# A DLRM tower with all pair products: 256 of the 780 pairs laid out with samples on partitions, and the batch in five blocks

## What is computed

```
e = stack of tbl_f[ids[:, f]] for the 40 fields          # (2048, 40, 64), f32
vi, vj = e[:, i_idx, :], e[:, j_idx, :]                   # 780 pairs i < j
z = einsum('bpe,bpe->bp', einsum('bpd,pde->bpe', vi, W), vj)
h = concatenate([z, dense_ctx], axis=1)                   # 796 columns
h = maximum(h @ W_top1 + b_top1, 0)                       # 796 -> 512
h = maximum(h @ W_top2 + b_top2, 0)                       # 512 -> 256
y = h @ W_top3                                            # 256 -> 1
```

## Time and profile before

| | before |
|---|---|
| median of 3 runs | 1374.25 us (1374.18 to 1374.57) |
| the profiled execution, its time | 1374.48 us |
| its span, from first to last instruction | 1372.7 us |
| PE busy | 1307.9 us (95%) |
| DVE busy | 928.9 us (68%) |
| POOL busy | 604.8 us (44%) |
| ACT busy | 83.4 us (6%) |
| mean granted TensorE clock | 0.994 of 2.4 GHz |

### The profile page before, as it was taken

The page is one execution under the profiler, slowest core; times in us unless marked ns, Lnnn a source line. Parts: engine busy times, 40 slices in busy tenths (PEclk is TensorE's granted clock), DMA queues, the critical chain, the costliest instruction groups (busy, mean ns, idle before and its releaser), DMA issues.

```text
span 1372.7 us, 17118 instructions
## 1 busy us (share of the span) xinstructions
PE 1307.9 (95%) x7024; PEld 463.4 (34%) x7024; DVE 928.9 (68%) x804; ACT 83.4 (6%) x137; POOL 604.8 (44%) x646
## 2 busy tenths in 40 slices
PE   0699999998999999999999999999999999999998
PEld 0233333332333333333333333333333333333333
DVE  0378877776634788788854588878873478888860
ACT  0000000000000000000000100000000000000001
POOL 6777777777777777754543444451000000000000
PEclk9899999999999999999999999999999999999999
DMA  4233332222222233322211222222110011111100
GB/s 163 42 73 73 70 69 73 73 66 65 65 42 58 66 74 72 74 66 63 65 45 37 47 66 62 62 64 53 47 40 23 23 48 51 50 47 47 32 1 0
DMA packets 49782, 77.38 MB, mean 56 GB/s; under 512 B 13540, under 2 KB 13540, under 8 KB 49576
## 3 DMA queue, kind: packets, MB, share of 16 engines
q1 hardware_dynamic: 29216, 55.26, 13.6%
q0 software_dynamic: 20480, 21.01, 8.4%
q10 hardware_dynamic: 8, 0.01, 0.0%
HBM read 76.22 MB, written 0.01 MB: 56 GB/s over the span
## 4 chain that ended last, share of the span: by engine, by line
PE 86%; POOL 9%; issue 3%; DMA 1%; ACT 1%; POOLq 0%
PE u_ps L311 48%; PE z_ps L328 25%; POOL rows L268 9%; PE turn_ps L342 6%; PE turn_ps L294 3%; PE turn_ps L347 2%; PE u_ps L342 1%; PE u_ps L313 1%; PE u_ps L347 1%; PE turn_ps L351 0%; DMA rows<-in_tbl,ids_all 0%; ACT h_sb L418 0%; DMA ids_all<-in_ids 0%; PE u_ps L351 0%; ACT y_row L424 0%
## 5 line engine op out<-in xcount | busy, mean ns | idle before, releaser
L388 DVE TENSOR_TENSOR prod<-u_ps,x 128x1024 f32<-128x1024 f32 x800 | 928.2, 1218 | 401.8 <-PE u_ps L313 398.4
L313 PE MATMUL u_ps<-x,w_ring 64*128 64x512 f32 x1600 | 759.9, 610 | 0.0
L311 PE MATMUL u_ps<-x,w_ring 64*128 64x512 f32 x1600 | 759.9, 610 | 0.0
L268 POOL DMA_INDIRECT rows<-in_tbl,ids_all x640 | 604.1, 944 | 326.9 <-issue 196.1
L311 PEld LDWEIGHTS u_ps<-x,w_ring 64*128 64x128 f32 x1600 | 279.9, 187 | 420.4 <-issue 324.9
L328 PE MATMUL z_ps<-prod,ones 128*32 128x512 f32 x3200 | 393.4, 601 | 0.0
L313 PEld LDWEIGHTS u_ps<-x,w_ring 64*128 64x128 f32 x1600 | 279.8, 187 | 0.0
L328 PEld LDWEIGHTS z_ps<-prod,ones 128*32 128x32 f32 x3200 | 85.6, 109 | 279.7 <-issue 152.4
L294 PE MATMUL turn_ps<-ident,rows 128*128 128x128 f32 x320 | 53.9, 293 | 60.3 <-DMA rows<-in_tbl,ids_all 54.3
L407 ACT COPY x<-turn_ps 128x512 f32<-128x512 f32 x80 | 46.9, 586 | 635.8 <-PE turn_ps L294 635.8
L342 PE MATMUL turn_ps<-z_sb,mlp_sb 128*128 128x512 f32 x182 | 81.5, 599 | 0.8 <-ACT z_sb L412 0.8
(11 more groups left out here) (19 smaller groups left out, 14.7 us busy)
## 6 DMA issues: line engine op xcount, KB each, us to landing
w_ring<-in_w_pair SPq DMA_DIRECT2D x200, 256.0 KB, 2.7
rows<-in_tbl,ids_all POOLq DMA_INDIRECT x640, 2.5
mlp_sb<-in_mlp SPq DMA_DIRECT2D x1, 2308.0 KB, 11.5
ids_all<-in_ids SPq DMA_DIRECT2D x1, 320.0 KB, 3.3
z_sb<-in_dense_t SPq DMA_DIRECT2D x4, 32.0 KB
out_y<-y_row ACTq DMA_DIRECT2D x4, 2.0 KB
```

The source lines that it names most:

```text
L268: nc.gpsimd.indirect_dma_start(rows[:, slot, s, par * DIM:(par + 1) * DIM], None, tables[f], bass.IndirectOffsetOnAxis(ap=ids_all[:, SUB * ...
L311: pe.matmul(u_ps[:, bank, :], w_ring[0:DIM, c % W_SLOTS, cols], x[0:DIM, b % 2, n_even, :], start=True, stop=True)
L313: pe.matmul(u_ps[:, bank + 1, :], w_ring[DIM:P, c % W_SLOTS, cols], x[DIM:P, b % 2, n, :], start=True, stop=True).then_inc(mains_done, 1)
L388: nc.vector.tensor_tensor(prod[:, full % PROD_SLOTS], u_ps[:, bank:bank + 2, :], other, ALU.mult).then_inc(prods_done, 1)
```

## The change

The batch goes through in five blocks, of 256, 512, 512, 512 and 256 samples. Each block has 136 units as before, called standing (F, and D for the pairs inside duos). The other pairs, those between each of the 16 duos 4 to 19 and the 8 fields of duos 0 to 3, 256 in all, are done in moving units (R). There the operands change places: 128 samples of `x` stand in the array, and the eight matrices of a field, 512 columns, move through. A moving unit does 128 samples and 16 pairs. A block of 512 has 64 of them (four times 16), one of 256 has 32. Its products (L555) are made with the gathered rows themselves, which stay in `kept`, and lie in `rprod` with samples on partitions, so that the sum over the 64 numbers of a field runs along the columns. That sum is one instruction of VectorE (L578), or sixteen of ScalarE with 64 columns each (L614). VectorE takes the first 24 moving units and then every fourth, 82 in all, and ScalarE 174. The 256 sums of a sample are turned around by TensorE in two pieces a block (`zr`, L484), and ScalarE copies them to `z_sb` (L624). TensorE's sums (L473) are left for the standing units, 34 groups a block, and come at least three units after their group. `z_sb` keeps seven chunks (five and two).

`prod` becomes `fprod` (8 slots) and `rprod` (4 slots), `rows` has 6 slots, the weights come through 4 slots for standing and 3 for moving units. `x` is a ring of 28 duos, and 12 duos of the next block are turned within a block. Pieces of the layers lie six units apart.

```diff
-BLOCK = 512
+SIZES = [256, 512, 512, 512, 256]
+KEEP = 4
+X_SLOTS = 28
+WF_SLOTS, WR_SLOTS = 4, 3
+ROW_SLOTS = 6
+FPROD_SLOTS, RPROD_SLOTS = 2 * GROUP, 4
+SUM_LAG = 3
+def block_units(b):
+    moving = [("R", n, s) for n in range(KEEP, DUOS) for s in range(SUBS[b])]
+    ...
+def on_vector(u):
+    r = R_AT[u]
+    return r < 24 or r % 4 == 3
+MLP_AT = {3: ("zr", 0), 5: ("zr", 1), 16: ("l1", 0), 22: ("l1", 1), 28: ("l1", 2), 34: ("l1", 3),
+          40: ("l2", 0), 46: ("l2", 1), 52: ("l3", 0)}
+    free = 116 if b == 0 else 70          # duos_before_unit: the next block's 12 duos
+    for n in range(EARLY_DUOS):
+        at.setdefault(free + (len(UNITS[b]) - 4 - free) * n // EARLY_DUOS, []).append((b + 1, n))
 # TensorE, a unit
+    if kind == "R":
+        op = pe.matmul(u_ps[:, bank + half, :], x[on, x_slot(b, n), k * P:(k + 1) * P],
+                       wr_ring[on, c % WR_SLOTS, :], start=True, stop=True)
 # VectorE, a unit
+    if kind == "R":
+        nc.vector.tensor_tensor(rprod[:, r % RPROD_SLOTS], u_ps[:, bank:bank + 2, :],
+                                kept[:, b % 2, k:k + 1, :].to_broadcast([P, 2, KEPT * DIM]), ALU.mult)
 # VectorE's sum, one product later
+        nc.vector.tensor_reduce(zb[:, s, at:at + 2 * KEPT],
+                                rprod[:, r % RPROD_SLOTS].rearrange("p h (j d) -> p (h j) d", d=DIM),
+                                AX.X, ALU.add).then_inc(vsums_done, 1)
 # ScalarE's sum
+        for j in range(2 * KEPT):
+            one = rprod[:, slot, j // KEPT, j % KEPT * DIM:(j % KEPT + 1) * DIM]
+            op = nc.scalar.activation(one, one, ACT.Copy, accum_out=zb[:, s, at + j:at + j + 1])
+            op.then_inc(asums_done, 1)
```

More of the change, by code:

```diff
@@ L23, with standing_units @@
 BLOCK = 512
-SUB = BLOCK // P
 H1, H2 = 512, 256
 M1, M2 = H1 // P, H2 // P
+SIZES = [256, 512, 512, 512, 256]
+NB = len(SIZES)
+STARTS = [sum(SIZES[:b]) for b in range(NB)]
+SUBS = [n // P for n in SIZES]
+KEEP = 4
+KEPT = 2 * KEEP
 GROUP = 4
-W_SLOTS = 8
-ROW_SLOTS = 10
+X_SLOTS = 28
+WF_SLOTS, WR_SLOTS = 4, 3
+ROW_SLOTS = 6
 U_SLOTS = 3
-PROD_SLOTS = 2 * GROUP
-def unit_list():
-    units = []
+FPROD_SLOTS, RPROD_SLOTS = 2 * GROUP, 4
+SUM_LAG = 3
+def standing_units():
+    out = []
     for n in range(DUOS):
@@ L38, in unit_list @@
         if n % 2:
[L39 to L47, removed]
+            out.append(("D", n, n - 1))
+        out += [("F", n, k) for k in range(KEEP if n >= KEEP else 0, n)]
+    return out
+STANDING = standing_units()
+NF = len(STANDING)
+GROUPS = NF // GROUP
+NT = 2 * NF
 Z_TILES = 64
 K_GROUPS = Z_TILES // (2 * GROUP)
-ZK = -(-NT // Z_TILES)
-Z_LAST = NT - Z_TILES * (ZK - 1)
+ZF = -(-NT // Z_TILES)
@@ L52 @@
+Z_LAST = NT - Z_TILES * (ZF - 1)
 DENSE_ROW = 96
-FIRST_UNIT = {n: min(q for q, u in enumerate(UNITS) if u[1] == n) for n in range(1, DUOS)}
-FIRST_UNIT[0] = 0
+R_DUOS = DUOS - KEEP
+R_PAIRS = R_DUOS * 2 * KEPT
+ZR = R_PAIRS // P
+ZK = ZF + ZR
 W1_COLS, W2_COLS = ZK * H1, M1 * H2
+assert NF % GROUP == 0 and R_PAIRS % P == 0
+def block_units(b):
+    moving = [("R", n, s) for n in range(KEEP, DUOS) for s in range(SUBS[b])]
+    out, f, r = [], 0, 0
+    while f < NF or r < len(moving):
+        reach = DUOS if f >= NF else STANDING[f][1]
+        due = f >= NF or (r < len(moving) and f >= 8 and r * (NF - 20) <= (f - 8) * len(moving)
+                          and moving[r][1] <= reach)
+        if due:
+            out.append(moving[r])
+            r += 1
+        else:
+            out.append(STANDING[f])
+            f += 1
+    return out
@@ L77, in tile_pairs, with moving_pair, lay_standing, lay_moving @@
     return (i, j), (i, j + 1)
-def lay_w_pair(w):
+def moving_pair(n, half, j):
+    return 2 * (DUOS - 1 - n) + half, 2 * (DUOS - 1 - j // 2) + j % 2
+def lay_standing(w):
     out = np.zeros((GROUPS, P, GROUP, P), np.float32)
-    for q, (what, _, _) in enumerate(UNITS):
+    for f, (kind, _, _) in enumerate(STANDING):
         for half in range(2):
-            for par, pair in enumerate(tile_pairs(q, half)):
+            for par, pair in enumerate(tile_pairs(f, half)):
                 if pair is not None:
[L89 to L92, removed]
+                    one = w[pair_index(*pair)]
+                    out[f // GROUP, half * DIM:(half + 1) * DIM, f % GROUP, par * DIM:(par + 1) * DIM] = (
+                        one.T if kind == "D" and half == 1 else one)
     return out.reshape(GROUPS, P, GROUP * P)
+def lay_moving(w):
+    out = np.zeros((R_DUOS, P, KEPT, DIM), np.float32)
+    for n in range(KEEP, DUOS):
+        for half in range(2):
+            for j in range(KEPT):
+                out[n - KEEP, half * DIM:(half + 1) * DIM, j] = w[pair_index(*moving_pair(n, half, j))]
+    return out.reshape(R_DUOS, P, KEPT * DIM)
 def lay_mlp(w1, b1, w2, b2, w3):
@@ L156, in dlrm_tower @@
[L156 to L161, removed]
+        for n in range(EARLY_DUOS, DUOS):
+            at.setdefault(max(0, min(first[n] - 3, 8 + 7 * (n - EARLY_DUOS))), []).append((b, n))
+    if b + 1 < NB:
+        free = 116 if b == 0 else 70
+        for n in range(EARLY_DUOS):
+            at.setdefault(free + (len(UNITS[b]) - 4 - free) * n // EARLY_DUOS, []).append((b + 1, n))
@@ new lines, in duos_before_unit, with work_order @@
+    return at
+MLP_AT = {3: ("zr", 0), 5: ("zr", 1), 16: ("l1", 0), 22: ("l1", 1), 28: ("l1", 2), 34: ("l1", 3),
+          40: ("l2", 0), 46: ("l2", 1), 52: ("l3", 0)}
+def work_order():
+    order, sums = [], []
+    for b in range(NB):
+        duos = duos_before_unit(b)
+        for q in range(len(UNITS[b])):
+            u = UNIT0[b] + q
+            while sums and sums[0][0] <= u:
+                order.append(("sum", *sums.pop(0)[1:]))
+            order += [("duo", *d) for d in duos.get(q, [])]
+            if b and q in MLP_AT:
+                order.append((MLP_AT[q][0], b - 1, MLP_AT[q][1]))
+            order.append(("unit", b, u))
+            f = F_AT.get(u)
+            if f is not None and f % GROUP == GROUP - 1:
+                sums.append((u + 1 + SUM_LAG, b, f // GROUP - GROUPS * b))
+    order += [("zr", NB - 1, c) for c in range(ZR)]
+    order += [("sum", *s[1:]) for s in sums]
+    order += [(what, NB - 1, m) for what, m in MLP_AT.values() if what != "zr"]
+    return order
@@ L162, in dlrm_tower @@
+def dlrm_tower(nc, dense_t, ids, tables, mlp_w, w_standing, w_moving, out, N_DENSE):
+    order = work_order()
+    turn_at = {ev: t for t, ev in enumerate(ev for ev in order if ev[0] in ("duo", "zr", "l1", "l2", "l3"))}
     first_tail = turn_at["l1", NB - 1, 0]
+    for at, ev in enumerate(order):
+        if ev[0] == "duo" and DUOS * ev[1] + ev[2] >= X_SLOTS:
+            old = divmod(DUOS * ev[1] + ev[2] - X_SLOTS, DUOS)
+            assert ("unit", old[0], last_use(*old)) in order[:at], ev
@@ L295, in duo @@
+                pe.wait_ge(landed, total)
+                for s in range(SUBS[b]):
+                    op = pe.transpose(bank[:, s * P:(s + 1) * P], of[:, s, :], ident[:])
                 op.then_inc(turned, 1)
[L297 to L303, removed]
-                    pe.wait_ge(turn_read, turn_at["duo", b, n] + 1)
[L306 to L314, removed]
+            copied = set()
@@ L395, in _ @@
+            due = []
+            for what, b, u in order:
+                if what == "unit":
+                    products(u)
+                    if due:
+                        sum_over_d(due.pop())
+                    if u in V_AT:
+                        due.append(u)
+            for u in due:
+                sum_over_d(u)
         @block.scalar
@@ L433, in _ @@
                     duo(b, n)
+                elif what == "unit" and n in A_AT:
+                    sum_over_d(n)
+                elif what == "zr":
+                    move_zr(b, n)
                 elif what == "sum":
```

314 lines of the change are left out of this document (206 added, 108 removed).

## The result

| | before | after |
|---|---|---|
| median | 1374.35 us | 1420.21 us |
| the profiled execution's span | 1372.7 us | 1418.3 us |

A forecast was written before the change was run, and what follows sets the result against it. The prediction took TensorE to set the pace from 376 us on, and GpSimd's gathers up to about 362. TensorE alone 1293.5 + handover 18 + waits 46 = 1357.5 us of span, forecast 1359 us, range 1325 to 1410.

The forecast's parts named there:

- The start: Block 0: GpSimd's 176 gathers decide; the last awaited duo is turned from 225.7 us and block 1 begins at 232.3.
- TensorE alone, 295.5 us a block: A block of 512 with nothing else: 326.9 less 33.0 for removed sums plus 1.6 for `zr` pieces.
- ScalarE's sum: One 64-column activation with accumulator on ScalarE: 0.215 us, bounded by 0.11 below and 0.586 above.
- S: Time of the sixteen ScalarE sums of one moving unit, taken as 3.4 us.
- The walk through the waits, 13.8 us a block: At layer pieces TensorE waits for duo copies behind ScalarE's sums: 4.4, 5.6, 1.9, 1.9 us; 46 us in all.
- The handover to VectorE, 5 us a block and 18 in all: When sums begin on TensorE, VectorE idles about 0.25 us a group, the two engines being level; 3 us in block 4.
- The sum: Whole kernel: 1293.5 for TensorE alone + 18 handover + 46 waits = 1357.5 us of span, against 1372.7.
- The five blocks: No separate price; within TensorE's 1293.5 us: start 232.3, blocks 279.2, 295.5, 292.5, 168.5, end 25.5.
- ScalarE as the bound: Rival, slower: a ScalarE sum costs 0.32 us, S = 5.1, waits grow to 22.7; about 1437 us, chance 0.22.
- VectorE holds TensorE up: Rival: each group of sums loses 0.7 us rather than 0.25, 30 us more than the 18; about 1385, chance 0.08.

The follow-up runs named there:

- defer: The changed kernel with ScalarE taking each sum three units later in its order (before a layer piece at the latest), all work done: 1352.5 us.
- both_short: As act_short, and VectorE too sums only one of sixteen in its 82 moving units, the rest left out: 1331.1 us.
- warm: The changed kernel with six extra useless matmuls before the first two layer pieces of each block but the last: 1408.1 us.
- act_short: The changed kernel with ScalarE doing one of the sixteen activations of each of its 174 moving units, the rest left out: 1356.5 us.
- four_defer6: The changed kernel with four blocks of 512, ScalarE's sums three units later, and VectorE summing every sixth moving unit instead of every fourth: 1309.2 us.

## Why the prediction was wrong, step by step

*The start:* right but for 1.8 us. Duo 11 of block 1 is turned at 225.34 us and block 1's first unit starts at 234.10; 225.7 and 232.3 were forecast. Most of the 1.8 is again the clock behind a wait: TensorE had stood 4.63 us for that duo's rows, and the next three units, of 256 samples, took 2.86 us, where units of that size take 0.43 each at full clock.

*TensorE alone, 295.5 us a block:* near, but partly by luck. A moving unit costs what a standing one does, 0.86 us (one starts at 612.37 us and the next unit at 613.23). The 33.0 us taken off for 16 groups of sums are some 30.7 in the traces: runs of units are still broken 59 times a block, against 64 before, because layer pieces that came right behind a group's sums now stand alone. What makes up for it is that the 2.2 us of TensorE's waits in the block before, which the 295.5 kept, went away. No run came down to the 295.5: it is 307.6 us in defer and 304.2 in both_short.

*ScalarE's sum:* 0.24 us measured, 0.215 taken. S = 3.85 in place of 3.4, which lay within the forecast's bounds and did not decide; ScalarE would be full at S = 4.5 by the sum's own terms ((14.4 - 0.8)/3), not 4.6. The page "ScalarE: Activation LUTs" of the Trainium skill (What ACT_TABLE_LOAD costs) gave an estimate of 0.15 for an activation without the accumulator; the measured distance is 0.09 longer, and no run has such activations without the accumulator's read, so its share is not shown. The 224 cycles + N that the page "VectorE: DVE Perf Modes" of the Trainium skill (The TRN2 errata) states gave S = 3.8: the trace has 0.241 us an activation, which agrees.

*The walk through the waits, 13.8 us a block:* the mechanism was right, down to the places. Measured were 5.36, 6.00, 2.4 and 2.4, together 16.2, for 4.4, 5.6, 1.9 and 1.9.

*What stood nowhere: the clock behind a wait.* This is the first of the two steps that failed. The prediction priced a wait at its length. Behind it the pieces took 2.5, 2.95 and (at layer 2, 5.40 against 3.70) 1.7 us longer, 7.2 us in block 2's stage, and some 20 us over all layer pieces of the kernel. The warm run shows it as a cost by itself. I had read the profile's clock as full and treated it as given, when the change was about to bring waits that the kernel before did not have.

*The handover to VectorE, 5 us a block and 18 in all:* the second step that failed, and the larger one. 328.9 - 295.5 - 16.2 - 7.2 leaves 10.0 us a block, as do defer's 307.6 - 295.5 - 2.2 = 9.9. The trace of the changed kernel shows where they lie. Four stops in block 2's stage, of 1.2, 1.3, 0.7 and 0.7 us beyond the usual distance of two units' records, end with a product of VectorE: 3.8 us. Some 6.4 more are 71 places inside runs of units where the next record starts 0.03 to 0.17 us late; the kernel before has none of either. In both_short one stop of 0.3 is left, but 65 of the small delays (6.0 us). So the stops hang on VectorE's sums; what makes the small delays no run shows. Over the kernel such stops add up to 22 us and such delays to 26, together 48 where 18 were forecast. The prediction spread the loss evenly, at 0.25 us a group, and averaged both engines over a cycle of four moving units; the stops come where the order puts a sum of VectorE ahead of a product that TensorE's next unit waits for. In the last block it is the same: from its first layer piece to the end the change takes 195.9 us, defer 192.1, act_short 190.1 and both_short 185.0.

*The sum:* the four stages from the first layer piece on took 313.8, 328.9, 318.1 and 195.9 us, where the prediction's terms, cut at the same places, give 298.0, 314.3, 300.3 and 185.6, and 1.8 us more stand before them. That is 60 us: some 15 to 18 in each full block and 10 in the last. Over the kernel some 30 of them are the handover, 20 the clock, 8 the longer waits for copies and 2 the start.

*The five blocks:* never priced as an edit of their own. Their terms were in the sum, so this did not miss the number; but I compared the whole with the kernel before and did not see that four blocks would be 42 us faster.

*The rivals:* the slower one, ScalarE as the bound at 0.32 us a sum, did not come about: the time lies near its side, but the cause was refuted by defer and four_defer6, in which ScalarE does as much or more in less time. The rival that VectorE holds TensorE up, with 30 us more than the 18 and a chance of 0.08, is what came in size (48 us), as stops and small delays rather than as 0.7 us at each group; its 1385 is too low, since the clock and the longer waits stand beside it. The range, up to 1410, had the price of ScalarE's rival thinned out at its top and nothing for the clock.

## What to carry to other kernels

When long runs of small instructions move to an idle engine, look first at what short service that engine already gives the busy one, and put that service ahead of the runs: here the order of one engine, with no work saved, was worth 68 us. A wait on TensorE can cost more than its length: behind the waits of 5 to 6 us here the matmuls ran at the lower clock for 2 to 3 us of extra time; price both. Where two engines come out level, the average over a cycle says little: TensorE stood 26.9 us for VectorE's products, and 5.7 once VectorE's sums were short. And a change in two parts is to be priced in two parts, each against the kernel without it: here the one part gains 4.2% once ordered, and the other costs some 2.7 to 3% under either order.

## What the runs showed of the hardware

A ScalarE activation with an accumulator is two instructions, 0.241 us and 0.187 us for 64 columns, and they overlap so that the pair repeats every 0.24 us. TensorE's clock fell at every wait of 5.3 to 6.0 us before a layer piece, and at some of 2.4 us: the eight records behind the one before layer 2 took 5.40 us in place of 3.70 (the granted clock is 0.50 from 659.2 us, a microsecond after that wait ended), while the four behind the one before layer 3 took 1.88, as without a wait. In a stretch filled with matmuls of no use the clock stayed at 1.00. A unit of two matmuls with samples in the array and weights moving through costs the same 0.86 us as the other way around.
